# Attention behind a token network: another order of one pair's work on TensorE, ScalarE, VectorE and GpSimd

## The reference

```python
def attention(x):                       # x = layernorm(h): [64, 141, 64]
    q, k, v = split(x @ W_qkv.T)        # 8 heads of 8 channels
    attn = einsum('bhqd,bhkd->bhqk', q, k) * (8 ** -0.5 * temperature)
    attn = softmax(where(local_mask, attn, -inf))
    return einsum('bhqk,bhkd->bhqd', attn, v) @ W_proj.T + b_proj
def ffn(x):                             # x = layernorm(h), one routed expert per sequence
    h = relu(x @ Wi.T + bi)
    for l in range(2):
        h = relu(shared_l(h) + routed_l(h) + h)
    return h @ Wo.T + bo
h = h + attention(layernorm(h))
h = h + ffn(layernorm(h))
```

## Time and profile before

| | |
|---|---|
| time, median of 3 runs | 3182.53 us (3173.91 to 3184.05) |
| the profiled execution | 3178.7 us, its span 3176.9 us |
| attention stage | from about 2608 to 3177 us of the span |
| PE busy in the whole span | 2820.0 us (89%) |
| DVE, ACT, POOL busy | 2086.8, 2075.8, 2115.6 us |
| busy in the attention stage (569 us) | PE 491.79 us; DVE 404.31, POOL 326.76, ACT 315.82 |
| busy in 32 us of its loop (2864 to 2896) | PE 29.50 us, DVE 24.35, POOL 20.11, ACT 19.53; granted clock of PE 1.00 |

### The profile page before, as it was taken

One profiled execution on the slowest core, in us unless ns is written; L12 is line 12 of the kernel. 1 busy time (PEld: TensorE's weight loads), 2 busy tenths in 40 slices (PEclk: granted clock), 3 DMA queues, 4 the chain that ended last, 5 costly groups with the idle time before them and its releaser, 6 DMA issues. The chain is left out here.

```text
span 3176.9 us, 199484 instructions
## 1 busy us (share of the span) xinstructions
PE 2820.0 (89%) x85132; PEld 1925.4 (61%) x85132; DVE 2086.8 (66%) x3770; ACT 2075.8 (65%) x3500; POOL 2115.6 (67%) x1099
## 2 busy tenths in 40 slices
PE   6886999997899997799999689999999978999997
PEld 4555777775677776577777434444444425766665
DVE  7775888883688885588888344444444436777775
ACT  4663777773577775477776167777777764665664
POOL 3773999993899996599999244544445425666664
PEclk9997999998899999899999789999999998999998
DMA  5764666664466664466665411111112113111110
GB/s 159 229 224 152 180 183 185 183 184 137 142 185 183 179 184 159 135 184 187 182 179 159 132 47 57 58 59 56 59 52 61 50 26 78 31 30 30 30 30 24
DMA packets 237216, 379.88 MB, mean 120 GB/s; under 512 B 117378, under 2 KB 155074, under 8 KB 236818
## 3 DMA queue, kind: packets, MB, share of 16 engines
q1 hardware_dynamic: 225410, 363.99, 38.3%
q10 hardware_dynamic: 7920, 10.03, 1.0%
q0 software_dynamic: 3744, 3.84, 0.9%
HBM read 217.93 MB, written 159.83 MB: 119 GB/s over the span
## 5 line engine op out<-in xcount | busy, mean ns | idle before, releaser
L1490 POOL TENSOR_TENSOR rstd<-var,mhalf 128x16 f32<-128x16 f32 x512 | 1554.9, 3057 | 643.9 <-DVE var L1245 643.1
L1259 DVE TENSOR_TENSOR zt<-ps,rstd 128x512 f32<-128x512 f32 x512 | 345.2, 684 | 81.4 <-POOL rstd L1490 78.6
L547 PEld LDWEIGHTS ps<-cwl,hc 64*64 64x64 f32 x16384 | 273.4, 139 | 203.5 <-issue 203.5
L1245 DVE TENSOR_REDUCE var<-sq 128x16 f32<-128x528 f32 x384 | 267.9, 698 | 189.5 <-ACT sq L903 173.8
L530 PE MATMUL ps<-zb,ex 48*128 48x512 f32 x1024 | 300.8, 662 | 52.5 <-DVE zt L1259 22.9
L594 PE MATMUL ps<-ident,hp 128*128 128x128 f32 x1536 | 277.1, 304 | 46.7 <-ACT ho L928 41.5
L1080 ACT ACTIVATE a<-ps,fc1b 128x1024 f32<-128x1024 f32 x256 | 271.4, 1111 | 64.6 <-PE ps L816 64.6
L547 PE MATMUL ps<-cwl,hc 64*64 64x64 f32 x16384 | 309.2, 226 | 0.0
L558 PEld LDWEIGHTS ps<-dyi,gt 64*48 64x48 f32 x16384 | 215.7, 125 | 140.4 <-issue 140.3
L1316 DVE TENSOR_TENSOR zt<-zt,gbx 128x512 f32<-128x512 f32 x384 | 296.5, 772 | 5.6
L618 PE MATMUL ps<-dx,hp 128*32 128x24 f32 x24576 | 271.9, 193 | 31.4 <-issue 29.0
(11 more groups left out here) (200 smaller groups left out, 4847.5 us busy)
## 6 DMA issues: line engine op xcount, KB each, us to landing
h_scratch<-ho SPq DMA_DIRECT2D x256, 512.0 KB
hc<-h_scratch SPq DMA_DIRECT2D x256, 512.0 KB, 4.4
wsb<-in_w SPq DMA_DIRECT2D x64, 288.0 KB
gin<-g_scratch SPq DMA_DIRECT2D x252, 72.0 KB
gin<-g_scratch SPq DMA_DIRECT2D x504, 36.0 KB
wc<-expert_scratch SPq DMA_DIRECT2D x64, 129.0 KB, 2.6
g_scratch<-hp SPq DMA_DIRECT2D x32, 192.0 KB, 3.9
g_scratch<-hp ACTq DMA_DIRECT2D x32, 192.0 KB, 4.3
```

The costliest lines, as they stand in the source:

```text
L547: last = nc.tensor.matmul(main_ps(s, h, u)[64 * m:64 * m + 64, r:512:8], hc[b][k, 8 * h + r, 64 * m:64 * m + 64], cwl[k], start=False, sto ...
L1245: nc.vector.tensor_reduce(dst, src, axis=AX.X, op=ALU.add).then_inc(var_ready, 1)
L1259: nc.vector.tensor_tensor(by_px(zt[h][:, u]), by_px(main_ps(s, h, u)), scale, ALU.mult).then_inc(norm_ready, 1)
L1490: nc.gpsimd.tensor_tensor(rstd[u][:], var[u][:], mhalf[:], ALU.pow).then_inc(rstd_ready, 1)
```

## The change

No instruction is added or removed in a pair's work, and no buffer or semaphore changes. `front2` and `qk_copy` are split into a key half and a query half, and the calls in `step` are put into another order on four engines. Line numbers of the changed kernel are up to 11 higher.

```diff
@@ tensor: front2 is split @@
-            def front2(i, p):
+            def front2_k(i, p):
                 g = num(i, p)
                 pe.wait_ge(xT_ready, g + 1)
                 at_least(pe, v_ready, g)
                 nc.tensor.matmul(fr_ps[1][:, 0:2 * TOK], wk[:], xT[:, :, 0:TOK], start=True, stop=True).then_inc(k_psr, 1)
+
+            def front2_q(i, p):
+                pe.wait_ge(xT_ready, num(i, p) + 1)
                 nc.tensor.matmul(fr_ps[0][:, 0:2 * TOK], wq[:], xT[:, :, 0:TOK], start=True, stop=True).then_inc(q_psr, 1)
@@ tensor: step @@
                 if c := at(i, p, b, 1):
                     turn(*c)
+                if b == 1 and old:
+                    back_layer(old[0], old[1], 0)
                 if b == 1 and prev:
                     back_o(*prev[0:2])
-                if b == 1 and old:
-                    back_layer(old[0], old[1], 0)
-                if b == 2 and old:
-                    back_out(*old[0:2])
+                if b == 2 and nxt:
+                    front3(*nxt[0:2])
                 if c := at(i, p, b, -1):
                     scores(*c)
                 if b == 0 and nxt:
                     front1(*nxt[0:2])
+                if b == 0 and old:
+                    back_y(*old[0:2])
                 if c := at(i, p, b, 1):
                     values(*c)
-                if b == 0 and old:
-                    back_y(*old[0:2])
                 if b == 0 and nxt:
-                    front2(*nxt[0:2])
+                    front2_k(*nxt[0:2])
                 if b == 0 and old:
                     back_in(*old[0:2])
-                if b == 1 and nxt:
-                    front3(*nxt[0:2])
+                if b == 0 and nxt:
+                    front2_q(*nxt[0:2])
                 if b == 1 and prev:
                     back_proj(*prev[0:2])
                 if b == 1 and old:
                     back_layer(old[0], old[1], 1)
+                if b == 2 and old:
+                    back_out(*old[0:2])
@@ scalar: step, behind pT_copy, xT_copy, yT_copy and oT_copy @@
+                if b == 1 and nxt:
+                    k_copy(*nxt[0:2])
                 if b == 1 and old:
                     relu_layer(old[0], old[1], 0)
+                if b == 2 and nxt:
+                    v_copy(*nxt[0:2])
+                if b == 2 and old:
+                    relu_layer(old[0], old[1], 1)
                 if here:
                     exp(i, p, b)
-                if b == 0 and nxt:
-                    qk_copy(*nxt[0:2])
                 if b == 0 and old:
                     relu_in(*old[0:2])
-                if b == 1 and nxt:
-                    v_copy(*nxt[0:2])
-                if b == 1 and old:
-                    relu_layer(old[0], old[1], 1)
+                if b == 0 and nxt:
+                    q_copy(*nxt[0:2])
@@ vector: step @@
                 if here:
                     with_mask(i, p, b)
-                if b == 0 and old:
-                    norm_end(yn, rs2, rs2_ready, yn_ready, num(old[0], old[1]))
                 if b == 0 and nxt:
                     norm1_end(*nxt[0:2])
                 if here:
                     row_max(i, p, b)
+                if b == 0 and old:
+                    norm_end(yn, rs2, rs2_ready, yn_ready, num(old[0], old[1]))
                 if b == 0 and (c := at(i, p, 0, 9)):
                     final(*c[0:2])
-                if b == 0 and prev:
+                if b == 1 and prev:
                     o_norm(*prev[0:2])
+                if b == 1 and nxt2:
+                    norm1(*nxt2[0:2])
                 if b == 2 and prev:
                     residual(*prev[0:2])
-                if b == 2 and nxt2:
-                    norm1(*nxt2[0:2])
@@ gpsimd: step @@
                 if here:
                     shift(i, p, b)
-                if b < 2 and nxt:
-                    keys(nxt[0], nxt[1], b)
-                if b == 2 and prev:
-                    power(va2, rs2, va2_ready, rs2_ready, *prev[0:2])
+                if b == 1 and nxt:
+                    keys(nxt[0], nxt[1], 0)
+                    keys(nxt[0], nxt[1], 1)
                 if b == 2 and nxt2:
                     power(va1, rs1, va1_ready, rs1_ready, *nxt2[0:2])
                 if b == 2 and prev:
                     with_bias(*prev[0:2])
+                    power(va2, rs2, va2_ready, rs2_ready, *prev[0:2])
```

More of the change, by code:

```diff
@@ L1872, in _ @@
             front1(0, 0)
-            front2(0, 0)
+            front2_k(0, 0)
+            front2_q(0, 0)
             front3(0, 0)
@@ L1920, in xT_copy, with k_copy @@
                                ).then_inc(xT_ready, 1)
-            def qk_copy(i, p):
+            def k_copy(i, p):
                 g = num(i, p)
@@ L1926, in qk_copy, with q_copy @@
                 nc.scalar.copy(kT[:].rearrange("d m n -> d (m n)"), fr_ps[1][:, 0:2 * TOK]).then_inc(k_ready, 1)
-                act.wait_ge(q_psr, g + 1)
+            def q_copy(i, p):
+                act.wait_ge(q_psr, num(i, p) + 1)
                 nc.scalar.copy(qT[p][:, :, 0:TOK], fr_ps[0][:, 0:2 * TOK].rearrange("d (m n) -> d m n", m=2)
@@ L1967, in _ @@
             xT_copy(0, 0)
-            qk_copy(0, 0)
+            k_copy(0, 0)
+            q_copy(0, 0)
             v_copy(0, 0)
```

## The result

The changed kernel takes 3129.45 us (median of 4 runs, 3122.12 to 3140.69) against 3181.95 us (4 runs, 3173.91 to 3184.05) before: ratio 0.9843, 95% interval 0.9808 to 0.9878. The profiled execution happens to be the slowest of its four, 3140.69 us with a span of 3138.9 us: its token network, which the change does not touch, ended later than that of the profile before. So the two traces are compared within the attention stage alone, from its first instruction on DVE (the memset of `xs`) to the end of the span: 3176.9 - 2609.0 = 567.9 us before, 3138.9 - 2622.0 = 516.9 us after, 51.0 us less. In the tables a "period" is worked out as in the prediction, from the first and the last start of the 96 shifts, times 3/95; it includes the lighter first pairs.

The account below looks back on a forecast made before the run. PE was its own bound except for stalls of 1.61 us a pair; less 0.11, the 1.50 over 31 intervals gave 46.5 us, 45 with head and tail: 3178.7 to 3134, stated as 3136 us; range 3126 to 3166 us.

Parts of the forecast that it names:

- PE's stalls of 1.61 us a pair: PE late at three places at a pair's start: scores 0.70, front1 0.17, turn 0.74 us; all were to go.
- the 0.11: Estimate in us a pair, taken back from 1.61 for the loop's branch on DVE, POOL and ACT, leaving 1.50.
- 45: Predicted saving in us from the profiled 3178.7: 46.5 over 31 intervals, with a loss of 1.5 for head and tail.
- The walk on PE: PE's new order timed from the turn of block 1 with nothing late, reaching the turn of block 0 at 9.65 us.
- The new chain over keys and the shared port: From turn of block 0 through keys, shift, second norm, mask and back_y to the next: 14.22 us against PE's 14.49.
- Rival 2: Shift gets the port before yn's norm_end, making back_y late: chain 16.08 us, no change, 3178 us; chance 0.09.
- The load of xs: SP's chain from residual through issue, landing (3.89 us), norm1, mask and row_max: 14.09 us, below PE's 14.49.
- a sign of being wrong: DVE's st waiting for the DMA of xs, listed among the observations that would show the forecast wrong.
- the origin of the stalls: norm1's 1.66 us on DVE between second norm and mask, named as origin of the 0.70 and 0.74 us stalls.

## Why the prediction was right

**PE's stalls of 1.61 us a pair, and that all three go.** Right. The loop's pair in the earlier trace rows of 16.10 us became 14.47, 1.63 less, 0.02 more than the stalls; the 0.11 that I took back for the loop's branches was an estimate that no run shows, and nothing of it appears in the pairs. That, and the head and tail, is the difference between 45 and the 51.0 us of the stage.

**The walk on PE.** Right: front3 at 0.87 us (0.97 predicted), scores 2.17 (2.27), turn 4.57 (4.70), scores 5.59 (5.67), front1 6.55 (6.63), turn 9.67 (9.65).

**The new chain over keys and the shared port, 14.22 us, with 0.27 to spare.** It did not bind: back_y starts 0.31 or 0.47 us behind final's end, where a back_y that waits starts 0.15 behind it, so 0.16 and 0.32 us are to spare. The port itself is nearer: norm_end 0.3 us later, behind shift, costs the gain. Rival 2 was the right mechanism, with the right condition (which of the two starts first, by 0.10 us here; 0.17 by the prediction's rows, but 0.08 by the times in its walk, where shift lacks the handover). Its price of 1.6 us a pair was measured as 1.40. The Trainium skill, "SBUF — State Buffer", in "SBUF: two separate sides", says that whichever starts first holds the pair for its whole instruction. The trace agrees with it in that direction: norm_end took 1.89 us behind a shift. In the other it agrees only in part: the shift that started 0.10 us behind norm_end became 0.11 us longer, although 0.26 us of norm_end were left.

**The load of xs.** Its landing took 3.94 us from the end of the issue (2869.47 to 2873.41) against the 3.89 predicted from the earlier trace rows. But DVE's st does wait for this DMA in every pair, and the prediction had named that as a sign of being wrong. The sign was badly chosen: the run with the load first shows that the wait costs nothing. Without it, mu waits for shift instead.

**What the prediction had wrong without harm to its number.** It called norm1's place the origin of the stalls and costed its move as if a norm in the second third only met an idle DVE. The move alone loses 50 us: in the old order of POOL the norm collides with keys and shift. In its walk I had seen the port for the second norm and for yn, and for keys as a chain, but not as a collision with norm1. In the changed kernel the late k_copy keeps them apart, by 0.44 us in the pair shown; the prediction had not worked this out, so on this point its number came out right by luck. The gain belongs to the set: norm1 early, keys together and late, the first norm's power and norm_end first, o_norm out of the way.

## What to carry to other kernels

Where VectorE and GpSimd work on SBUF side by side, an order is read as one timetable of both: 0.35 us of VectorE work placed 0.3 us later cost 1.4 us a pair here. A single move of a reordering may lose what the set gains, so a part that looks harmful alone isn't evidence against the whole; walk the new order on all engines. When a variant is slower, look at the pairs one by one and at PE's granted clock in each, before its average is put down to the order. To learn whether an engine bounds a stretch, add a little work to it there: 0.59 us of matmuls cost 0.58 us a pair where PE bounded and nothing where it did not.

## What the runs showed of the hardware

- Beside a GpSimd instruction of 1.78 us (128x952), a VectorE `tensor_scalar` on 128x3 took up to 1.59 us instead of 0.17 and ended with it; a `tensor_tensor` with two SBUF inputs took 1.89 instead of 0.36 and ended 0.22 us behind it. The mask, which reads PSUM and SBUF, took 1.15 us beside keys in the changed kernel, as everywhere.
- In the other direction, shift took 1.89 us instead of 1.78 beside a norm_end that had started 0.10 us earlier. The small power instruction (128x3, 0.86 us) did not hold up a norm_end that started within it (0.35 us at 2877.51 in the kernel before); it took 1.02 us itself where the norm_end had started just ahead.
- A wait of 1.21 us on PE was followed by a granted clock of 0.50 in the stretch from 2893 to 2895 us, and the pair took 1.44 us more than its neighbours. Behind most stalls of the same length in the same trace the clock stayed at 1.00; in another kernel it fell in every second pair of most of the loop, behind a wait of 1.41 us (15.86 and 18.28 us a pair). No run shows what decides.
- A load from DRAM in two DMAs of 35 KB each had landed 3.9 us behind the end of its issue.
